# Split products that start with their high passes, high halves written by GpSimd, and a new timetable, in a four-block convolution and attention kernel

## The reference

```python
x = _L0_conv_ref(x, ...)   # batch norm, 3x3 depthwise conv, q/k/v, k and v resized to 7x7, attention with bias, 3x3 conv, 1x1, MLP
x = _L1_conv_ref(x, ...)   # group norm (8 groups), linear attention (softmax over k's channels and q's tokens), projection, + xn
x = _L2_conv_ref(x, ...)   # group norm (32 groups), 8-head attention over 196 tokens, projection, + x
x = _L3_conv_ref(x, ...)   # group norm (32 groups), single-head attention over 196 tokens, projection, + x
```

## Time and profile before

| | |
|---|---|
| Median of 3 runs | 2153.09 us (2151.42 to 2154.98) |
| The profiled execution | 2154.48 us, its span 2152.4 us |
| Mean granted TensorE clock | 0.977 of full speed |
| PE (TensorE matmuls) busy | 2037.7 us, 95% of the span, 15104 instructions |
| PEld (weight loads) busy | 1682.7 us, 78% |
| ACT (ScalarE) busy | 1847.4 us, 86% |
| DVE (VectorE) busy | 1825.9 us, 85% |
| POOL (GpSimd) busy | 1249.3 us, 58% |

### The profile page before, as it was taken

How to read it: one execution, slowest core, us unless ns; L and a number is a source line. 1 busy time by engine, 2 the same in 40 slices (tenths; PEclk the granted TensorE clock), 3 DMA queues, 4 the chain that set the end, 5 groups by cost and what they waited for, 6 DMA issues and landing times. The chain is left out here.

```text
span 2152.4 us, 59558 instructions
## 1 busy us (share of the span) xinstructions
PE 2037.7 (95%) x15104; PEld 1682.7 (78%) x15104; DVE 1825.9 (85%) x4617; ACT 1847.4 (86%) x6165; POOL 1249.3 (58%) x2954
## 2 busy tenths in 40 slices
PE   4678999999999999999999999999999999999976
PEld 3466788888888888888888888888888888887766
DVE  6778899898899999989999998999999899987532
ACT  2258999999999999999999999999999999998874
POOL 2454666666666666666666666666666666664311
PEclk9699999999999999999999999999999999999987
DMA  3000011011101100110111001001101110100000
GB/s 126 16 24 7 26 39 39 24 37 37 37 16 37 37 30 30 37 37 15 37 37 37 22 37 37 20 33 37 37 22 37 37 37 16 38 31 31 9 25 37
DMA packets 29822, 70.33 MB, mean 33 GB/s; under 512 B 6252, under 2 KB 7088, under 8 KB 29744
## 3 DMA queue, kind: packets, MB, share of 16 engines
q1 hardware_dynamic: 26928, 67.68, 8.7%
q10 hardware_dynamic: 2816, 1.72, 0.3%
HBM read 30.85 MB, written 12.85 MB: 20 GB/s over the span
## 5 line engine op out<-in xcount | busy, mean ns | idle before, releaser
L820 ACT ACTIVATE e<-ps_s,nm 98x196 f32<-98x196 f32 x1024 | 424.2, 437 | 69.6 <-DVE nm L956 69.4
L828 ACT ACTIVATE e<-e,rden 98x196 f32<-98x196 f32 x1024 | 413.3, 487 | 0.0
L592 POOL TENSOR_SCALAR xn<-x,gn_scale,gn_shift 128x196 f32<-128x196 f32 x384 | 314.1, 828 | 20.8 <-POOL gn_shift L587 20.8
L1152 DVE SCALAR_TENSOR_TENSOR y<-opad,w_dw,y 128x406 f32<-128x406 f32 x512 | 311.4, 660 | 0.0
L1133 DVE SCALAR_TENSOR_TENSOR y<-xpad,w_dw,y 128x406 f32<-128x406 f32 x512 | 298.0, 636 | 0.0
L956 DVE TENSOR_REDUCE nm<-ps_s 98x4 f32<-98x784 f32 x256 | 245.0, 969 | 43.7 <-PE ps_s L1160 43.7
L1209 PE MATMUL ps_s<-w_eye,e 98*98 98x98 f32 x2048 | 224.4, 250 | 10.2 <-ACT e L828 7.0
L834 ACT COPY pt<-ps_s 98x392 f32<-98x392 f32 x512 | 232.0, 505 | 1.9 <-PE ps_s L1209 1.8
L1209 PEld LDWEIGHTS ps_s<-w_eye,e 98*98 98x98 f32 x2048 | 193.9, 130 | 47.2 <-issue 35.9
L820 ACT ACTIVATION_READ_ACCUMULATOR e<-ps_s,nm 98x1 f32 x1024 | 224.3, 219 | 0.0
L570 POOL TENSOR_TENSOR gn_t<-gn_group 128x4 f32<-128x4 f32 x96 | 26.6, 277 | 321.4 <-DVE gn_group L1006 227.7
(11 more groups left out here) (226 smaller groups left out, 5670.0 us busy)
## 6 DMA issues: line engine op xcount, KB each, us to landing
x_in<-in_x SPq DMA_DIRECT2D x32, 392.0 KB, 3.8
x_res<-in_x SPq DMA_DIRECT2D x32, 392.0 KB, 3.3
x2b<-x SPq DMA_DIRECT2D x32, 392.0 KB, 2.8
out<-x SPq DMA_DIRECT2D x32, 392.0 KB, 2.6
out_pairs<-out SPq DMA_DIRECT2D x32, 392.0 KB, 2.4
w_q<-in_q SPq DMA_DIRECT2D x3, 256.0 KB
w_k<-in_k SPq DMA_DIRECT2D x3, 256.0 KB
w_v<-in_v SPq DMA_DIRECT2D x3, 256.0 KB
```

The lines of the kernel that those rows point to most:

```text
L592: g.tensor_scalar(dst[:, c, of_image(i)], src[:, c, of_image(i)], t.scale[:, j:j + 1], t.shift[:, j:j + 1], ALU.mult, ALU.add).then_inc(t. ...
L820: s.activation(e2[:, j, tc], tile(use)[0:HALF, of_image(tc)], ACT.Exp, bias=nm2[:, j, tc:tc + 1], accum_out=den2[:, 2 * i + tc, h:h + 1]). ...
L828: s.activation(e2[:, j, tc], e2[:, j, tc], ACT.Copy, scale=rden2[:, 2 * i + tc, h:h + 1]).then_inc(p2_done[j].sem, 1)
L1152: v.scalar_tensor_tensor(out=dst, in0=window(opad, c, k, CR), scalar=tap, in1=dst, op0=ALU.mult, op1=ALU.add).then_inc(conv2_steps.sem, 1)
```

## The change

- `split_product` becomes two functions. `by_highs` issues the four matmuls that need only the high half of the computed operand (it with the weights' high and low halves), `by_lows` the two with its low half. The wait for the highs stands before the first, the wait for the lows between them (in `hv`, before the first pair of low passes). For `proj` the highs' wait is on `a2_high`, the lows' on the banks read by DVE.
- POOL writes the high halves itself: behind the two `tensor_scalar` into `xn` of a chunk it runs the same two again with the fp32r tile as output. ACT's six casts per pair go. DVE's wait for a chunk's high counts both images.
- All five tables and `BANK_USES` are new. POOL's round keeps its order with all lags one higher. In DVE's round `low2_0` and `low2_1` now stand behind `stats1`, and `low1_0` stands 13 places behind the copy `gn1` (17 before). The step from `conv1_0` (first DVE step of a pair) to `o3_0` (its last) is 830 - 43 = 787 slots, before 790 - 14 = 776.

```diff
-                self.high = Count(f"gn{n}_high", KC)
+                self.high = Count(f"gn{n}_high", 2 * KC)
...
-            def normalized(p, n, src, dst):
+            def normalized(p, n, src, dst, high, readers):
...
                         g.tensor_scalar(dst[:, c, of_image(i)], src[:, c, of_image(i)], t.scale[:, j:j + 1],
                                         t.shift[:, j:j + 1], ALU.mult, ALU.add).then_inc(t.done.sem, 1)
+                    if c == 0 and has_before(p):
+                        pool.wait_ge(*full(p - 1, latest(*readers)))
+                    for i in range(2):
+                        j = 2 * c + i
+                        alone()
+                        g.tensor_scalar(high[:, 0, c, of_image(i)], src[:, c, of_image(i)], t.scale[:, j:j + 1],
+                                        t.shift[:, j:j + 1], ALU.mult, ALU.add).then_inc(t.high.sem, 1)
...
-                    for n, src, dst, readers in splits:
-                        for c in range(KC):
-                            p = pair_of(t, u, ACT_AT[f"high{n}_{c}"])
-                            if p is not None:
-                                act.wait_ge(gn[n].done.sem, gn[n].done.at(p, 2 * (c + 1)))
-                                if has_before(p):
-                                    act.wait_ge(*full(p - 1, latest(*readers)))
-                                s.copy(dst[:, 0, c], src[:, c]).then_inc(gn[n].high.sem, 1)
...
-                                dve.wait_ge(gn[n].high.sem, gn[n].high.at(p, c + 1))
+                                dve.wait_ge(gn[n].high.sem, gn[n].high.at(p, 2 * (c + 1)))
...
-            def split_product(dst, lhsT, rhs):
-
-                terms = [(k, a, b) for k in range(KC) for a, b in ((0, 0), (0, 1), (1, 0))]
-                for k, a, b in terms:
-                    ins = mm(dst, lhsT(a, k), rhs(b, k), (k, a, b) == terms[0], (k, a, b) == terms[-1])
+            def by_highs(dst, lhsT, rhs, part):
+
+                for n, (k, weight) in enumerate(itertools.product(range(KC), range(2))):
+                    a, b = (weight, 0) if part == "rhs" else (0, weight)
+                    mm(dst, lhsT(a, k), rhs(b, k), n == 0, False)
+
+            def by_lows(dst, lhsT, rhs, part):
+
+                for k in range(KC):
+                    a, b = (0, 1) if part == "rhs" else (1, 0)
+                    ins = mm(dst, lhsT(a, k), rhs(b, k), False, k == KC - 1)
                 return ins
...
                             pe.wait_ge(*free(p, use))
+                            pe.wait_ge(gn[1].high.sem, gn[1].high.at(p, 2 * KC))
+                            source = (tile(use)[0:HALF, :], lambda a, k: xs1[:, a, k, of_tile(j // 2, j % 2)],
+                                      lambda b, k: ws["kv1"][:, b, k], "lhsT")
+                            by_highs(*source)
                             pe.wait_ge(gn[1].low.sem, gn[1].low.at(p, KC))
-                            split_product(tile(use)[0:HALF, :], lambda a, k: xs1[:, a, k, of_tile(j // 2, j % 2)],
-                                          lambda b, k: ws["kv1"][:, b, k]).then_inc(filled(use), 1)
+                            by_lows(*source).then_inc(filled(use), 1)
```

More of the change, by code:

```diff
@@ L1 @@
+import itertools
 import numpy as np
@@ L38 @@
 SP_AT = {
-    "x": 0, "res": 230, "hop": 460, "hop_out": 691, "store": 793,
+    "x": -103, "res": 128, "hop": 486, "hop_out": 716, "store": 819,
 }
 PE_AT = {
[9 rows of a table removed]
[9 rows of a table added]
 }
 ACT_AT = {
[13 rows of a table removed]
[13 rows of a table added]
 }
 DVE_AT = {
[11 rows of a table removed]
[11 rows of a table added]
 }
 POOL_AT = {
-    "resize0": 16, "resize1": 32, "probs0": 80, "probs1": 96, "gn1": 256, "gn2": 320, "gn3": 560, "rows3": 624,
+    "resize0": 144, "resize1": 160, "probs0": 208, "probs1": 224, "gn1": 384, "gn2": 448, "gn3": 688, "rows3": 752,
 }
 BANK_USES = {
[5 rows of a table removed]
[5 rows of a table added]
 }
@@ L627, in step @@
                                 pool.wait_ge(*read(p - 1, use))
-                        normalized(p, 1, x1, xn1)
+                        normalized(p, 1, x1, *splits[0][1:])
                     p = pair_of(t, u, POOL_AT["gn2"])
@@ L636, in step @@
                             pool.wait_ge(*full(p - 1, latest("s3_0", "s3_1")))
-                        normalized(p, 3, x3, xn3)
+                        normalized(p, 3, x3, *splits[2][1:])
                     for c in range(KC):
@@ L1331, in step @@
                             pe.wait_ge(*free(p, use))
+                            pe.wait_ge(gn[1].high.sem, gn[1].high.at(p, 2 * KC))
+                            source = (tile(use)[:, 0:N2], lambda a, k: ws["q1"][:, a, k, of_chunk(c)],
+                                      lambda b, k: xs1[:, b, k], "rhs")
+                            by_highs(*source)
                             pe.wait_ge(gn[1].low.sem, gn[1].low.at(p, KC))
-                            split_product(tile(use)[:, 0:N2], lambda a, k: ws["q1"][:, a, k, of_chunk(c)],
-                                          lambda b, k: xs1[:, b, k]).then_inc(filled(use), 1)
+                            by_lows(*source).then_inc(filled(use), 1)
                     for i in range(2):
@@ L1362, in step @@
                                 pe.wait_ge(*free(p, use))
+                                pe.wait_ge(gn[2].high.sem, gn[2].high.at(p, 2 * KC))
+                                source = (tile(use)[:, 0:N2], lambda a, k: ws[f"{name}2"][:, a, k, of_chunk(c)],
+                                          lambda b, k: xs2[:, b, k], "rhs")
+                                by_highs(*source)
                                 pe.wait_ge(gn[2].low.sem, gn[2].low.at(p, KC))
-                                split_product(tile(use)[:, 0:N2], lambda a, k: ws[f"{name}2"][:, a, k, of_chunk(c)],
-                                              lambda b, k: xs2[:, b, k]).then_inc(filled(use), 1)
+                                by_lows(*source).then_inc(filled(use), 1)
                     for i in range(2):
@@ L1370, in step @@
                             pe.wait_ge(*free(p, use))
-                            pe.wait_ge(gn[2].low.sem, gn[2].low.at(p, KC))
+                            pe.wait_ge(gn[2].high.sem, gn[2].high.at(p, 2 * KC))
                             for tc in range(2):
-                                last = split_product(tile(use)[0:HALF, tc * CH:(tc + 1) * CH],
-                                                     lambda a, k: xs2[:, a, k, of_tile(i, tc)],
-                                                     lambda b, k: ws["v2"][:, b, k])
+                                source = (tile(use)[0:HALF, tc * CH:(tc + 1) * CH], lambda a, k: xs2[:, a, k, of_tile(i, tc)],
+                                          lambda b, k: ws["v2"][:, b, k], "lhsT")
+                                by_highs(*source)
+                                if tc == 0:
+                                    pe.wait_ge(gn[2].low.sem, gn[2].low.at(p, KC))
+                                last = by_lows(*source)
                             last.then_inc(filled(use), 1)
@@ L1390, in step @@
                             pe.wait_ge(*free(p, use))
-                            for source in elsewhere(use, *(f"av{g}" for g in range(GROUPS))):
-                                pe.wait_ge(*read(p, source))
-                            split_product(tile(use)[:, 0:N2], lambda a, k: ws["p2"][:, a, k, of_chunk(c)],
-                                          lambda b, k: as2[:, b, :, k]).then_inc(filled(use), 1)
+                            pe.wait_ge(a2_high.sem, a2_high.at(p, GROUPS))
+                            source = (tile(use)[:, 0:N2], lambda a, k: ws["p2"][:, a, k, of_chunk(c)],
+                                      lambda b, k: as2[:, b, :, k], "rhs")
+                            by_highs(*source)
+                            for low in elsewhere(use, *(f"av{g}" for g in range(GROUPS))):
+                                pe.wait_ge(*read(p, low))
+                            by_lows(*source).then_inc(filled(use), 1)
                     for j in range(4):
@@ L1400, in step @@
                             pe.wait_ge(*free(p, use))
+                            pe.wait_ge(gn[3].high.sem, gn[3].high.at(p, 2 * KC))
+                            source = (tile(use)[0:HALF, 0:CH + 2], lambda a, k: xs3[:, a, k, of_tile(j // 2, j % 2)],
+                                      lambda b, k: ws["v3"][:, b, k], "lhsT")
+                            by_highs(*source)
                             pe.wait_ge(gn[3].low.sem, gn[3].low.at(p, KC))
-                            split_product(tile(use)[0:HALF, 0:CH + 2], lambda a, k: xs3[:, a, k, of_tile(j // 2, j % 2)],
-                                          lambda b, k: ws["v3"][:, b, k]).then_inc(filled(use), 1)
+                            by_lows(*source).then_inc(filled(use), 1)
                     for c in range(KC):
@@ L1408, in step @@
                             pe.wait_ge(*free(p, use))
```

(7 more changed lines are left out.)

2 lines of the change are left out of this document (1 added, 1 removed), and 76 rows, old and new, of tables (ACT_AT, BANK_USES, DVE_AT, PE_AT).

## The result

The changed kernel takes **2227.49 us** (median of 3 runs, 2225.6 to 2228.2) against 2153.09 us: ratio 1.0336, 95% interval 1.0314 to 1.0359. I had forecast 2146 us with a range up to 2180 us: the direction was wrong and the time lies outside the range.

What follows compares the result with a forecast made beforehand. PE was taken as the bound (61.96 of 62.3 us a round). Terms -12 (new order), +3 (bare group-norm chains) and +2 (longer pair) gave -7 against the profiled 2154.5 us: 2147.5, or 2146 for the median; range 2126 to 2180 us.

Steps and rivals of the forecast that it cites:

- the longer way of a pair: Filling and draining: 787 slots for 776, but slots are only ranks; +2 us, ends -4 and +5.4.
- the DMAs: SP's queue: same five per round, x one lag earlier; nothing waited for them in steady rounds, so zero.
- Highs first: PE's split products: low-half passes last save one wait per round, at most 0.44 us a round.
- GpSimd's writes: POOL: twelve more a round at 0.86 us, 10.3 us; hidden in steady rounds, +3 us for first and last pairs.
- rival 3: POOL becomes the bound, above 1.11 us a write; 2187 us at 1.2 us a write; chance 0.12.
- What DVE pays: DVE slowed by twelve more POOL writes: +0.9 us a round, to 57.6 us, hidden behind PE.
- Rival 5: DVE held up by each POOL write for 0.51 us: 62.8 us a round, 2171 us; chance 0.03.
- The new order: Steady rounds: about half of PE's 0.8 us stalls recovered, 0.45 us a round over 26 rounds, -12 us.
- rival 4: DVE waits for POOL in its own queue at low1_0; PE loses 0.45 us a round, 2169 us; chance 0.12.
- Rival 1: All PE stalls go: 0.8 us in each of 26 rounds, -21 us, 2132 us; chance 0.09.
- Rival 2: Nothing gained: highs come too late or an equal new wait appears; 2153, at most 2157 us; chance 0.13.
- Rival 6: PE was not the bound (weight loads 83% busy); time follows DVE at 57.6 us, 2031 us; chance 0.02.

Runs made afterwards that it cites:

- e4: Kernel before with only the new order of the passes (high halves first), ACT still casting, old timetable: 2140.52 us, ratio 0.9926.
- e9: Kernel before with both the new order of the passes and GpSimd's writes, old timetable, DVE's loop at 963: 2150.90 us, ratio 0.9976.
- e1: Changed kernel with 37 semaphore increments at the start of DVE's program, moving its loop from 926 to 963: 2167.19 us, ratio 1.0058.
- e2: Kernel before with 219 increments at the start of DVE's program, moving its loop to 1182: 2195.1 us, ratio 1.0180.
- e10: Kernel before with 64 increments at the start of DVE's program, moving its loop to 1027: 2178.45 us, ratio 1.0108.
- e15: e1 with DVE's low half of gn1's second chunk moved behind the reads of proj (366 to 370): 2160.33 us, ratio 1.0026.
- e6: e1 with ACT's six casts back, placed by hand in its new table, and GpSimd's writes gone: 2240.23 us, ratio 1.0390.
- e16: e6 with gn1's two casts later (361, 368) and, as in e15, low1_1 behind proj's reads: 2166.89 us, ratio 1.0056.

## Why the prediction was wrong, point by point

The spans of the profiled executions, in the order in which one thing at a time is changed:

| kernel | span | 23 rounds | step, us |
|---|---|---|---|
| before | 2152.4 | 23 x 62.31 | |
| e4: highs first | 2140.6 | 23 x 62.02 | -11.8 (rounds -7) |
| e9: and GpSimd's writes | 2148.2 | 23 x 62.25 | +7.6 (rounds +5.5) |
| e1: and the new timetable | 2162.8 | 23 x 62.73 | +14.6 (rounds +11) |
| after: and the loop at 926 | 2225.0 | 23 x 65.38 | +62.2 (rounds +61) |

By the ratios of medians, each to the kernel before on its own chip, the four steps are -0.74%, +0.50%, +0.82% and +2.8 to +3.0%, or -16, +11, +18 and 60 to 64 us: a span is one execution, and the small steps are known to some us only.

- **The step that failed is a term that was put at nothing.** For the longer way of a pair the prediction says that "the slots are only ranks", as the section on the kernel before has it that the tables set nothing but an order, and it put the DMAs at zero, since nothing waited for them. So the sum had no term for where an engine's loop lies. But a lag more or less also changes how many instructions stand ahead of the loop: on DVE 963 before, 926 now. In place of that nothing the runs showed a stop of 2.70 to 2.93 us at DVE's branch in each of 23 rounds, 62 us in all. e1 shows that it is the place alone, e2 and e10 that the kernel before has the stop too when it is moved. No rival covered it. The trace of before had what was needed for the question: the packets of instructions during filling and draining, none in the steady rounds.
- **Highs first.** "Worth at most 0.44 us a round": it was 0.29, and the wait of the earlier trace rows for DVE's low half went. Right in mechanism and size. The draining gained 5 us more (301.9 to 296.5 us behind the last jump back), which I had not counted; that its last products too have passes to do before the lows is the likely reason, not a tested one.
- **GpSimd's writes.** I took 0.86 us each. In the changed kernel the new ones took 0.77 and the old ones 0.88, in e9 0.51 and 1.01; POOL's busy time grew by 7.9 us a steady round, where I had 10.3. POOL didn't become the bound (rival 3 falls; it waits for others 7.6 us a round, 5.1 of them for `gn_group` and 2.6 for ACT's copies into `v3t`). But "costs nothing there as long as the order gives that distance" was wrong for the old timetable: from e4 to e9 the round grew by 0.23 us, +7.6 us in all where I had 3. PE's new waits there are for ACT's `e` (0.16 us a round) and `kv` (0.08); that the longer way from `gn_group` to the lows is what delays them is my reading and not shown.
- **What DVE pays.** I had +0.9 us a round. The low halves became shorter, not longer: 0.692 us in e9, in the same timetable as the 0.707 of the earlier trace rows, and 0.604 in the changed kernel; conv2's taps took 0.645 and 0.647 for 0.663. Rival 5 falls. The Trainium skill's rule on the shared port (SBUF — State Buffer, section Who interferes with whom) names the same pair of kinds; no run here shows DVE paying for twelve more GpSimd writes a round.
- **The new order.** The sum had one term of -12 for all stalls, those of the passes among them, and +2 for the longer way. The passes alone gave 11.8; the new tables gave nothing and cost 14.6. This is the second failure: I priced an order by the stalls it might remove and not by the cycle it makes. In e1 that cycle is PE for 38.5 us (1030.84 to the end of q3's product in bank e, for which ACT waits), ACT 3.8 (1069.54 to 1073.30, its last copy into `v3t`), POOL 17.6 (`rb`, gn1's chain, eight writes), DVE 1.9, PE again: with 1.0 us for the handovers 62.8 us, the round. That ACT's copies stand in it follows from the times and the kernel; no run has moved them. Its end has the form of rival 4, one place on: the reads of `proj` are queued behind a low half that waits for POOL. I had given that 0.12, and its 0.45 us a round is what e15 to e1 shows in part (0.25).
- **Rival 1** falls for the new timetable; it is the old one with highs first that comes near it, with 0.15 us of gaps in PE's busy time a round. **Rival 2** (nothing gained, another wait of PE's in place of the old) is the nearest to e1, where PE waits 0.84 us a round for `proj`'s reads; it was priced at a round of 62.3 us, and e1's is 62.73. **Rival 6** falls: in those rounds of e4 weight loads were busy 83% as before (1185 of 1433 us), and PE was the bound all the same.

On the stop itself the Trainium skill has a rule (Runtime: NRT & Kernel Launch, section Instruction fetch mechanics): a taken branch whose target isn't in the engine's current window of two pages forces a DMA of the target before execution goes on. The trace agrees with the mechanism, at 2.7 to 3.0 us a time. The Trainium skill gives there pages of 256 instructions in 16 KB; e10 disagrees with that size for VectorE, and the measurement decides: the packets that move at the stop are of 8 KB, and the places fit blocks of 128. The same section of the Trainium skill gives TensorE a store four times as large. PE's loop, which has 472 matmuls where DVE's has 333 instructions in all, does go round with 0.06 to 0.16 us at its branch, here in every run; that the size of its store is the reason isn't tested.

What stays open: the count of the window in blocks. "A loop that touches four blocks of 128 is fetched anew, one that touches three isn't" fits all six loops that were tried (963, 926, 1182 and 1027 on DVE; 402 and 252 instructions on SyncE), and the loops of ACT and POOL, which have at most 267 and 236 records a round in these traces and never stopped, don't speak against it; but where a block begins in the loaded program isn't known, so for DVE's 333 instructions the good starts are bounded and not pinned. Open too are 0.2 us a round of the new timetable, and 3.6 us of it at the ends.

## What to carry to other kernels

Where engines run a loop, look at each engine's branch in the trace: the time from it to the next instruction of its sequencer, and the bytes on the queue of instructions within steady rounds. If there are any, pad ahead of the loop or shorten it until there are none, and do so again after every edit that changes the code before the loop; otherwise an experiment measures the padding. Second, a step's value in a timetable is that of the cycle it lies on: an instruction that waits makes everything queued behind it wait too (the two casts of e6, 2.9 us a round). To place waiting steps later helped there and in e15, but not in e16, so each move has to be measured. And where a view names a releaser, look in the kernel whether the step waits for it at all.

## What the runs showed of the hardware that I had not expected

- A loop of 333 instructions on VectorE costs 0.22 to 0.26 us or 2.7 to 3.0 us at its branch, by its place alone: 37 instructions' difference ahead of it was 60 us in 23 rounds, 2.8% of the kernel. On SyncE 402 instructions in the loop cost 2.39 to 2.70 us, and 252 cost 0.23 to 0.28.
- What such a stop costs went with the work that the engine still had when it came: with taps and a row maximum of 0.96 us ahead, DVE idled for 1.3 (e2) of 2.8 us and the round grew by 1.2 us; with a reciprocal of 0.17 us ahead, DVE idled for 2.7 and the round was 2.65 us longer. The timetables differ too, so the work ahead is the likely reason and not the only difference.
- Of two GpSimd writes of one shape, right behind each other, those to `xn` took 1.01 us and those to the high half 0.51 us in e9, where `xn` alone took 0.86 before. The cause wasn't tried.
